# A local-attention stack with VectorE's rotations and ScalarE's squares reordered, and the sum of k's squared halves made in PSUM

## The reference, cut to what matters

```python
qkv = x @ Wqkv
q, k, v = jnp.split(qkv, 3, -1)              # 16 heads of 64
q = l2norm(q) * qs;  k = l2norm(k) * ksc
q = q * cos * scale + rotate_half(q) * sin * scale
k = k * cos * inv + rotate_half(k) * sin * inv
out = local_attention(q, k, v)               # windows of 32 queries, 64 keys
return out.transpose(0, 2, 1, 3).reshape(b, n, INNER) @ Wo
```

## Time and profile before

| what | value |
|---|---|
| runs of the kernel | 4605.27 us median of 3 (4597.25 to 4605.72) |
| the profiled execution | 4604.19 us, its span from first to last instruction 4602.4 us |
| mean granted TensorE clock | 0.969 |
| local stack, from the trace | about 590 to 3880 us, 48 batches |
| one batch of it, undisturbed | 68.10 us |

### The profile page before, as it was taken

One profiled execution on the slowest core, in us unless ns is written; L12 is line 12 of the kernel. 1 busy time (PEld: TensorE's weight loads), 2 busy tenths in 40 slices (PEclk: granted clock), 3 DMA queues, 4 the chain that ended last, 5 costly groups with the idle time before them and its releaser, 6 DMA issues. The chain is left out here.

```text
span 4602.4 us, 118671 instructions
## 1 busy us (share of the span) xinstructions
PE 4223.8 (92%) x47556; PEld 2343.2 (51%) x47556; DVE 3527.3 (77%) x3768; ACT 2286.6 (50%) x3572; POOL 2730.5 (59%) x3512
## 2 busy tenths in 40 slices
PE   7999979999999999999999999999999998688997
PEld 3333345555555555555555555555555555322333
DVE  5777568888788888888788888788778886467774
ACT  1666635445445545545445545445445444146664
POOL 0111177787777777787687777777777775111213
PEclk6999989999999999999999999999999999779999
DMA  3222032222222232222232223222232223122220
GB/s 89 55 54 56 27 86 59 59 64 72 70 64 58 59 80 67 59 66 59 71 75 57 60 65 83 58 65 61 59 73 61 59 63 77 40 57 52 50 41 19
DMA packets 169987, 282.19 MB, mean 61 GB/s; under 512 B 45996, under 2 KB 68076, under 8 KB 163820
## 3 DMA queue, kind: packets, MB, share of 16 engines
q1 hardware_dynamic: 142156, 241.93, 22.5%
q10 hardware_dynamic: 27648, 37.79, 3.3%
HBM read 62.03 MB, written 17.56 MB: 17 GB/s over the span
## 5 line engine op out<-in xcount | busy, mean ns | idle before, releaser
L1161 DVE SCALAR_TENSOR_TENSOR x<-l_r,l_qkvec,l_tab 128x1024 f32<-128x1024 f32 x768 | 939.8, 1279 | 35.4 <-ACT l_sq L1046 33.4
L551 DVE TENSOR_REDUCE a_nmax<-a_pair 128x2 f32<-128x1024 f32 x512 | 609.0, 1220 | 217.7 <-PE a_pair L674 217.6
L451 ACT ACTIVATE a_pt<-a_st 128x512 f32<-128x512 f32 x1024 | 543.3, 603 | 265.8 <-PE a_st L658 260.5
L971 POOL TENSOR_TENSOR l_ntmp<-l_seed 128x128 f32<-128x128 f32 (+1 forms) x480 | 173.6, 362 | 560.3 <-ACT l_seed L1027 541.5
L999 POOL TENSOR_TENSOR l_u<-x 128x512 f32<-128x512 f32 x384 | 499.4, 1301 | 0.0
L400 POOL CAST a_rparts<-a_rows 8x512 bf16<-8x512 f32 x32 | 19.3, 603 | 808.7 <-ACT a_rows L461 808.7
L998 POOL TENSOR_TENSOR l_u<-x 128x512 f32<-128x512 f32 x384 | 498.4, 1298 | 0.0
L1448 PE MATMUL l_r<-l_pbd,l_va 128*64 128x160 f32 (+1 forms) x6144 | 445.0, 298 | 40.3 <-DMA l_pbd<-l_pt 32.5
L1337 PE MATMUL l_r<-xs,l_wqkv 128*128 (+1 forms) x768 | 399.1, 611 | 67.1 <-DVEq L1246 59.5
L1004 POOL TENSOR_TENSOR l_p<-l_p,l_srec 128x1024 f32<-128x1024 f32 x192 | 365.3, 1903 | 150.9 <-POOLq L67 91.4
L1448 PEld LDWEIGHTS l_r<-l_pbd,l_va 128*64 128x64 f32 x6144 | 399.5, 138 | 100.6 <-issue 82.3
(11 more groups left out here) (203 smaller groups left out, 7357.4 us busy)
## 6 DMA issues: line engine op xcount, KB each, us to landing
l_kbd<-l_kn SPq DMA_DIRECT2D x768, 128.0 KB, 2.4
l_pbd<-l_pt SPq DMA_DIRECT2D x768, 64.0 KB
l_pbd<-l_pt ACTq DMA_DIRECT2D x576, 64.0 KB
a_ks<-a_scr SPq DMA_DIRECT2D x96, 192.0 KB
a_qs<-a_scr SPq DMA_DIRECT2D x288, 64.0 KB
a_scr<-a_parts SPq DMA_DIRECT2D x48, 256.0 KB, 2.5
l_pbd<-l_pt SPq DMA_DIRECT2D x192, 56.0 KB
l_wqkv<-in_wqkv SPq DMA_DIRECT2D x6, 1536.0 KB, 7.1
```

Of the source, the lines that this page charges most:

```text
L451: nc.scalar.activation(pt[n % 2][:, r, :], st[(4 * n + r + par) % 3][:], ACT.Exp, scale=SC).then_inc(exp_done, 1)
L551: nc.vector.tensor_reduce(out=nmax[:, n, 2 * i:2 * i + 2], in_=pair[i][:], op=ALU.max, axis=AX.X, negate=True).then_inc(pair_dve[i], 1)
L1161: last = nc.vector.scalar_tensor_tensor(out=t[a][:, 2 * half:2 * half + 2, :], in0=R[a][:, half, :].unsqueeze(1).to_broadcast([D, 2, T]), ...
```

## The change

For steps 0 to 2, DVE makes the rotation of q's first half ahead of the softmax transpose, then k0, q1, k1 behind it; before rotating k0 it waits until POOL has read all of the step before (`halves_of_pool(0)`). ACT squares k0 and k1 ahead of q1. In step 3 the orders stay. POOL adds the halves of q only. PE adds k's halves itself: eight products of `block8[:, 1]` with the two halves of `sq[1]`, behind a new semaphore `sqk_ready`, ahead of the wait for POOL's sum, then four for q: twelve where eight were. ACT drains twice instead of once.

```diff
-        sqs = [sb(f"sqs{a}", [D, T]) for a in range(2)]
+        sqs = sb("sqs", [D, T])
...
-                        nc.gpsimd.tensor_tensor(sqs[0][:], sq[0][:, 0, :], sq[0][:, 1, :], ALU.add)
-                        nc.gpsimd.tensor_tensor(sqs[1][:], sq[1][:, 0, :], sq[1][:, 1, :], ALU.add).then_inc(S["sq_sum"], 1)
+                        nc.gpsimd.tensor_tensor(sqs[:], sq[0][:, 0, :], sq[0][:, 1, :], ALU.add).then_inc(S["sq_sum"], 1)
...
-                        act.drain().then_inc(S["sq_ready"], 1)
...
                         if b is not None:
+                            square_k()
                             square_q(1)
-                            square_k()
+                            act.drain().then_inc(S["sq_ready"], 1)
+                            act.drain().then_inc(S["sqk_ready"], 1)
...
-                def rotate(a):
-
-                    halves_of_pool(1)
+                def rotate(a, half):
+
                     squared = S["q_dve"] if a == 0 else S["k_dve"]
-                    for half in range(2):
-                        v.wait_ge(squared, seen.next(squared))
-                        last = nc.vector.scalar_tensor_tensor(out=t[a][:, 2 * half:2 * half + 2, :],
...
+                    v.wait_ge(squared, seen.next(squared))
+                    last = nc.vector.scalar_tensor_tensor(out=t[a][:, 2 * half:2 * half + 2, :],
...
+                    if half == 1:
+                        last.then_inc(S["rq_ready"], 1)
+                        unread["ra"] += 1
+                        nc.vector.engine_nop().then_inc(S["r0_dve"] if a == 0 else S["r1_dve"], 1)
...
                     if has_ss:
                         read_norm()
+                    if b is not None and c < 3:
+                        halves_of_pool(1)
+                        rotate(0, 0)
                     transpose_p(c)
...
-                    if b is not None:
-                        rotate(0)
-                        rotate(1)
+                    if b is not None and c < 3:
+                        halves_of_pool(0)
+                        rotate(1, 0)
+                        rotate(0, 1)
+                        rotate(1, 1)
+                    elif b is not None:
+                        halves_of_pool(1)
+                        rotate(0, 0)
+                        rotate(0, 1)
+                        halves_of_pool(1)
+                        rotate(1, 0)
+                        rotate(1, 1)
...
                         claim(3)
+                        pe.wait_ge(S["sqk_ready"], seen.next(S["sqk_ready"]))
+                        for half in range(2):
+                            for k in range(NT):
+                                nc.tensor.matmul(R[3][32 * k:32 * k + 2 * CH, 0, 0:D], block8[:, 1, :], sq[1][:, half, 128 * k:128 * k + 128],
+                                                 start=False, stop=False, skip_group_check=True)
                         pe.wait_ge(S["sq_sum"], seen.next(S["sq_sum"]))
-                        for a in range(2):
-                            for k in range(NT):
-                                last = nc.tensor.matmul(R[3][32 * k:32 * k + 2 * CH, 0, 0:D], block8[:, a, :], sqs[a][:, 128 * k:128 * k + 128],
-                                                        start=False, stop=(a == 1), skip_group_check=True)
+                        for k in range(NT):
+                            last = nc.tensor.matmul(R[3][32 * k:32 * k + 2 * CH, 0, 0:D], block8[:, 0, :], sqs[:, 128 * k:128 * k + 128],
+                                                    start=False, stop=True, skip_group_check=True)
```

More of the change, by code:

```diff
@@ L1153, in halves_of_pool @@
                         unread["ra"] -= 1
-                def rotate(a):
-                    halves_of_pool(1)
+                def rotate(a, half):
                     squared = S["q_dve"] if a == 0 else S["k_dve"]
-                    for half in range(2):
-                        v.wait_ge(squared, seen.next(squared))
-                        last = nc.vector.scalar_tensor_tensor(out=t[a][:, 2 * half:2 * half + 2, :],
[L1162 to L1167, removed]
+                    v.wait_ge(squared, seen.next(squared))
+                    last = nc.vector.scalar_tensor_tensor(out=t[a][:, 2 * half:2 * half + 2, :],
+                                                          in0=R[a][:, half, :].unsqueeze(1).to_broadcast([D, 2, T]),
+                                                          scalar=qkvec[par][:, 2 * a + half:2 * a + half + 1],
+                                                          in1=tab[:, 2 * a:2 * a + 2, :], op0=ALU.mult, op1=ALU.mult)
+                    if half == 1:
+                        last.then_inc(S["rq_ready"], 1)
+                        unread["ra"] += 1
+                        nc.vector.engine_nop().then_inc(S["r0_dve"] if a == 0 else S["r1_dve"], 1)
                 def add_to_kept(batches):
```

## The result

The changed kernel takes 4617.82 us (median of 6 runs, 4603.67 to 4625.89) against 4603.61 us for the kernel before on the same chip (6 runs, 4597.25 to 4605.72): the ratio is 1.0031, with an interval of 1.0019 to 1.0042. It is slower by 0.3%, where 0.3% faster was forecast. The profiled execution took 4617.62 us, with a span of 4615.8. Further down, the medians of fit, b_unfit and b_pad include one far slower execution each (6052, 17012 and 5379 us), and their ratios don't.

The account below looks back on a forecast made before the run. PE was taken as nearly full, step 1 as ending on DVE. 36 batches at -0.43 us, rounded to -15, and +2 us for 12 others gave -13 us: 4592 us, eight in ten within 4581 to 4612.

Parts of the forecast that it names:

- the band as the bound at 4624 us: Rival: the later transpose delays the DMA-written band, PE reaches step 2 later, the kernel gets slower; 4624 us, 15%.
- three signs of being wrong: Band waited for by 0.6 us or more in step 1; step 2 not growing; GpSimd's L1004 starting after DVE's reciprocal.
- Step 1: Second step of a batch, ending on DVE: the rotation fills DVE's wait for L1004; -0.79 us.
- Step 0: First step of a batch: the added products stand on PE's path, so DVE's maximum starts later; +0.08 us.
- Step 2: Third step of a batch: PE runs without a gap, so the four added products cost fully; +0.28 us.
- Step 3: Last step of a batch: the added products fall into PE's 0.57 us wait for the output copy; 0.
- nothing, unless a satisfied wait between two groups costs: PE's added wait for k's squares, satisfied long before, costs nothing; bounds 0 and 0.05 us.
- Worth 0 by itself and a condition of the gain: GpSimd's dropped addition, 1.26 us: no gain alone, but it keeps GpSimd from becoming the bound.
- the chain is 13.19 us long: GpSimd runs 13.19 us without a wait, from L1004 to its last rotation half.
- it would become the bound 0.6 us earlier: With 0.79 us off DVE's path, GpSimd would become the bound 0.6 us earlier unless its addition went.
- The chance of 15% for "slower": The forecast's chance for a time above 4614 us; 15%.

Follow-up runs that it names:

- fit: The changed kernel with 32 and 80 idle PE drains between loops, so each batch loop touches eight instruction blocks; 4588.6 us, ratio 0.9981.
- b_unfit: The kernel before with 64 PE drains ahead of the loop of layers 2 and 4, meant to end inside a ninth block; 4604.7 us, ratio 1.0011.
- b_pad: The kernel before with 60 PE drains ahead of the loop of layers 2 and 4, ending just inside the eighth block; 4605.0 us, ratio 1.0014.
- rot_only: The kernel before with only the rotation of q's first half moved ahead of the transpose; 4575.3 us, ratio 0.9946.
- order_only: The kernel before with only the new DVE and ACT order; POOL keeps both additions, PE its eight products; 4556.9 us, ratio 0.9904.
- order_noact: order_only without ScalarE's three DMAs of the band, part of the attention not computed; 4544.9 us, ratio 0.9881.
- fit_onewait: fit without the semaphore for k's squares, its drain and wait; all twelve products behind the wait for POOL's sum; 4575.7 us, ratio 0.9960.
- fit_twosums: fit with POOL also adding k's halves, into a tile that nothing reads; 4577.8 us, ratio 0.9962.
- b_nine: The kernel before with 76 and 32 PE drains, so the loop of layers 2 and 4 touches nine instruction blocks; 4691.3 us, ratio 1.0192.

## Why the prediction was wrong

**The term that was missing.** The sum had no term for TensorE's own instructions beyond their execution. 65 more of them in each copy of the body moved the loop of layers 2 and 4 onto a ninth block, and that cost 29 us on the medians, 23 by the ratios: after against fit. Without it the forecast was near: fit is 9.7 us below the kernel before, drains included, where 13 were forecast. That nearness is partly luck. An undisturbed batch gained 0.30 us and not 0.43, since steps 2 and 3 cost more than forecast and step 0 gained what was to be a cost, and fit's interval reaches from 18 us to nothing. The rival that came closest in size, the band as the bound at 4624 us, had the right row (TensorE waits for the band in step 0) and the wrong reason: the band is late in 14 batches, where instructions are fetched, and waited for by 0.15 us in the others. With blocks of 256 and room for eight, a loop of 1812 instructions fits by my count unless it starts in the last 19 places of a block (b_unfit, at place 238, wasn't fetched, so the count isn't exact to the instruction), one of 1877 unless it starts in the last 84. The four loops of the kernel before start at places 89, 133, 175 and 220, of the changed one at 138, 56, 228 and 147: the third has gone over. A longer loop on the engine that is full should have been a rival with a chance of its own. None of the three signs of being wrong came in the undisturbed batch (the band is waited for by 0.15 us, step 2 grew, and GpSimd's division starts 0.1 us behind the reciprocal): all three looked only at such a batch, and the loss lay in the others.

**Step 1**, -0.79 forecast, -0.84 measured: right in mechanism and size. The wait for L1004 went, the wait of TensorE for `kn` fell from 1.24 to nothing (0.1 forecast), the band is waited for by 0.15 (0.3 forecast), and VectorE's rows follow each other as described.

**Step 0**, +0.08 forecast, -0.08 measured. Two terms were too large: the products are 0.22 and not 0.28 us, and VectorE's maximum starts 0.04 us after the end of the scores' row, not 0.14 (2508.73 against 2506.43 + 2.26):

```profile
2506.43 2.26 PE L1422 MATMUL l_r<-l_kbd,l_qn 64*32 64x128 f32 x128
...
2508.73 1.22 DVE L1245 TENSOR_REDUCE l_smax<-l_r 128x16 f32<-128x1024 f32 x1 [0.27 <-PE l_r L1422]
```

The 0.22 is 0.77 less 0.55, the pitches of the sums of squares in step 0 (0.78 in the step 1 shown above). The 0.14 and the 0.04 both rest on modelled ends. That k ahead of q1 gives something here was in the sum as a shift of the bound from VectorE to TensorE, and rot_only against order_only shows it: 0.27 us.

**Step 2**, +0.28 forecast, +0.48 measured. The products gave 0.22; the scores, at 2.43 instead of 2.17 us, the rest. That transfers moved by 0.5 us could slow a product of TensorE, and not only come late for it, was in no step. order_noact shows that it is ScalarE's transfers, where they run beside SyncE's.

**Step 3**, 0 forecast, +0.15 measured. The step that failed is "nothing, unless a satisfied wait between two groups costs", with its bounds of 0 and 0.05 us: fit_onewait puts the added signal and wait at 0.2 us a batch. The copy's wait fell as forecast, from 0.57 to 0.35.

**GpSimd.** "Worth 0 by itself and a condition of the gain" was half wrong. order_only and fit_twosums have both additions and the whole gain in step 1. The error is in the step from "the chain is 13.19 us long" to "it would become the bound 0.6 us earlier": a chain longer than its step only builds up a lag, over three steps some 0.9 us, and the rotation ahead of the transpose had just made room for 1.2. The condition is real only behind faster scores, as order_noact shows.

**The whole.** The change has two halves with opposite signs. The order is worth 1.0% (order_only). TensorE's half costs 0.7 us of the 1.0 that the order gains in each batch (67.12 against 67.80), and 23 to 29 us more through the place of the code. The chance of 15% for "slower" was too small mainly because only one mechanism stood behind it.

## What to carry to other kernels

Work taken off an engine that runs beside the critical path is worth nothing until a row shows someone waiting for it, while the same work on the engine that is full costs its time, its wait and whatever it pushes. When a loop of a full engine grows, count its instructions and the blocks that it touches before anything else, and look at the count of instruction packets on the page afterwards: here 119 or 233 said at once whether the code fits. Test the halves of a change apart; here one of them alone beats the kernel before by 1%.

## What the runs showed of the hardware

- TensorE's loop of 1812 or 1877 instructions brings 11 to 17 instruction packets in a layer when it touches eight blocks of 256, and 67 to 71 when it touches nine: then about nine a round. The price was 2.3 us a batch in the changed kernel and nearly 6 in b_nine (81 us in 14 batches), partly as gaps ahead of TensorE's first products, partly as later DMAs of the band.
- In b_nine, behind gaps of 2.2 to 2.8 us, TensorE's granted clock fell to its lower level (mean 0.96 over the fourteen batches), and 35 of the 81 us are the same records at that clock. In the changed kernel, with issue gaps of 0.3 to 1.3 us and waits for the band of up to 1.6 us, it fell in one batch of fourteen.
- The scores of a step, 128 records at the full clock, take 1.96 us from their start to the next row's with one of the two DMA queues writing, and 2.05 to 2.48 with both, depending on when they write.
- Four more products of 128 columns in four column groups take 0.22 us between two other groups.
- A semaphore with its drain and its wait, satisfied long before, cost 0.2 us in a batch of 67.8; each stands in every step, so it is the price of four.
